# Attention with a ternary feed-forward: output projections of two row blocks to one PSUM bank, and the written order of the attention passes laid out anew

## The reference

```
xn  = layernorm(x)                                  # x: 4 x 2048 x 256
att: q, k, v for 16 heads of 16 (half of q and k rotated by rope), causal softmax over 2048 keys
y   = softmax(q k^T / 4, causal) v                  # 4 x 2048 x 256
ffn: h = gelu(xn @ ternary(W_fc)^T); h = layernorm(h) * ln_w + ln_b; h @ ternary(W_proj)^T
out = x + y @ Wc + ffn
```

## Time and profile before

| | |
|---|---|
| median of three runs | 1917.17 us |
| profiled execution, its own time | 1912.73 us |
| its span, first to last instruction | 1910.9 us |
| TensorE matmul busy | 1832.3 us (96%) |
| VectorE busy | 1678.8 us (88%) |
| ScalarE busy | 1582.8 us (83%) |
| GpSimd busy | 538.3 us (28%) |
| mean granted TensorE clock | 0.972 of full speed |

### The profile page before, as it was taken

How to read it: one execution, slowest core, us unless ns; L and a number is a source line. 1 busy time by engine, 2 the same in 40 slices (tenths; PEclk the granted TensorE clock), 3 DMA queues, 4 the chain that set the end, 5 groups by cost and what they waited for, 6 DMA issues and landing times.

```text
span 1910.9 us, 41847 instructions
## 1 busy us (share of the span) xinstructions
PE 1832.3 (96%) x13879; PEld 695.6 (36%) x13879; DVE 1678.8 (88%) x4770; ACT 1582.8 (83%) x1916; POOL 538.3 (28%) x648
## 2 busy tenths in 40 slices
PE   6899999999879999999999999999999999999998
PEld 6555555565412222222332323222232322323223
DVE  5699999999779898999999999999999999999961
ACT  2477667666339999999999999999999999999994
POOL 0122112112151342415234241432414144241210
PEclk7899999999859999999999999999999999999999
DMA  4133333325333133140414314142341415323112
GB/s 177 32 95 104 88 88 102 106 75 117 102 80 66 22 58 49 31 64 22 81 35 80 58 44 64 44 95 30 72 59 43 67 40 94 43 59 64 35 40 74
DMA packets 160324, 129.01 MB, mean 68 GB/s; under 512 B 95344, under 2 KB 144752, under 8 KB 159768
## 3 DMA queue, kind: packets, MB, share of 16 engines
q1 hardware_dynamic: 160152, 126.88, 30.7%
HBM read 74.60 MB, written 42.98 MB: 62 GB/s over the span
## 4 chain that ended last, share of the span: by engine, by line
PE 45%; ACT 14%; issue 7%; DVE 5%; POOL 1%; SPq 1%; DMA 0%; DVEq 0%; ACTq 0%; POOLq 0%
PE pv L1570 18%; ACT prob L1352 12%; PE st L1555 10%; PE sm L1532 10%; PE sm L1503 4%; PE st L1542 2%; DVE sm L1433 2%; ACT excess L1345 1%; DVE sm L1421 1%; DVE pm L1438 1%; DVE pm L1421 0%; DVE pm L1433 0%; PE sm L1527 0%; ACT Y L1335 0%; POOL apart L1262 0%
## 5 line engine op out<-in xcount | busy, mean ns | idle before, releaser
L1352 ACT ACTIVATE prob<-st 128x1024 f32<-128x1024 f32 x1088 | 1047.7, 1029 | 62.7 <-PE st L1555 53.5
L1570 PE MATMUL pv<-prob,V 128*32 128x512 f32 (+3 forms) x5120 | 589.6, 542 | 5.6 <-POOL prob L1311 5.3
L1421 DVE CUSTOM_DVE_ANT_0 sm<-sm,mask 128x256 f32<-128x256 f32 (+3 forms) x1024 | 473.9, 521 | 39.2 <-PE sm L1532 35.0
L1532 PE MATMUL sm<-K,Q 48*128 48x512 f16 (+3 forms) x2112 | 479.8, 350 | 16.5 <-DVE pm L1421 6.9
L1555 PE MATMUL st<-Q,K 50*128 50x512 f16 (+3 forms) x2560 | 476.9, 353 | 13.9 <-ACT prob L1352 8.3
L1438 DVE TENSOR_REDUCE pm<-sm 128x1 f32<-128x512 f32 x640 | 412.6, 684 | 40.3 <-PE sm L1532 37.0
L1311 POOL TENSOR_SCALAR_AFFINE_SELECT prob<-prob 128x256 f32<-128x256 f32 (+1 forms) x448 | 190.4, 439 | 862.5 <-ACT prob L1352 857.7
L1433 DVE CUSTOM_DVE_ANT_0 sm<-sm,excess 128x512 f32<-128x512 f32 x448 | 301.3, 711 | 16.8 <-PE sm L1532 16.0
L1532 PEld LDWEIGHTS sm<-K,Q 48*128 48x128 f16 x2112 | 151.4, 95 | 325.6 <-DVE pm L1433 109.2
L1555 PEld LDWEIGHTS st<-Q,K 50*128 50x128 f16 x2560 | 125.2, 94 | 370.3 <-ACT prob L1352 270.4
L1345 ACT ACTIVATE excess<-st 128x1024 f32<-128x1024 f32 x218 | 220.6, 1025 | 9.1 <-DVE pm L1438 4.7
(11 more groups left out here) (169 smaller groups left out, 1938.1 us busy)
## 6 DMA issues: line engine op xcount, KB each, us to landing
Q<-scratch_q SPq DMA_DIRECT2D x102, 128.0 KB, 4.2
K<-scratch_k SPq DMA_DIRECT2D x102, 128.0 KB, 7.0
x<-in_x SPq DMA_DIRECT2D x16, 512.0 KB, 4.4
scratch_v<-Rt SPq DMA_DIRECT2D x64, 128.0 KB, 2.0
scratch_r<-Rt SPq DMA_DIRECT2D x16, 512.0 KB, 3.2
V_raw<-scratch_v SPq DMA_DIRECT2D x16, 512.0 KB, 10.0
Yc<-Y SPq DMA_DIRECT2D x124, 64.0 KB
spread<-scratch_i SPq DMA_DIRECT2D x124, 64.0 KB, 2.2
```

What stands on the lines that cost most here:

```text
L1352: act.activation(prob_of(quad, k)[:, :, :], st[number % ST][:, :, :], ACT.Exp).then_inc(exp_done, 1)
L1421: i = dve.tensor_tensor_reduce(x, x, mask[:, CH - block_width(t, k):], 1.0, -3e38, ALU.add, ALU.max, best(h, t, k))
L1532: i = pe.matmul(dst[:, at:at + width], lhsT=Q[slot][r, h // 2, t * P:(t + 1) * P], rhs=K[slot][r, h // 2, k * CH:k * CH + width], start=Tr ...
L1570: i = pe.matmul(pv[2 * DH * h:2 * DH * (h + 1), CH - width:CH], lhsT=V[quad % VSLOTS][:, j, h, :], rhs=prob_of(quad, u)[:, h % 2, at:at + ...
```

## The change

The four project entries of a pass become two: each fills one bank with two blocks of 128 tokens (four fp32 matmuls of 256 columns, eight records in the profile, one start flag per block), and one addition takes all 512 columns. In pass 15 the 16 late entries of chunks 12 to 15 become 8. A pass has 113 entries in place of 115. The order string is another one throughout. At the start of the stage, `load_kc(0)` and `place_ones(0)` go ahead of `load_v(0)`, `load_kc(1)` goes ahead of `load_m(0, 0, 0)`, `load_kc(quad)` waits for the second of the six difference operations of quad - 1 in place of the last, and on GpSimd the clearing of KC goes ahead of that of the ones, the differences of quad 0 ahead of the presetting of V, and the clearing of yn behind the differences of quad 1.

```
-PROJECT_AT = (64, 75, 87, 99)
+PROJECT_AT = (64, 87)
-    for s in reversed(range(SUB)):
-        sequence.insert(PROJECT_AT[s], ("project", s))
+    for a in reversed(range(HALVES)):
+        sequence.insert(PROJECT_AT[a], ("project", a))
-INVERT_EARLY, INVERT_LATE = LATE + 2, PROJECTS[2] + 1
+INVERT_EARLY, INVERT_LATE = LATE + 2, PROJECTS[1] + 1
 TIMETABLE = (
-    "wsmmswxmmwmsmsmmsmmswmmsmxwxmmsmwmxmsmmsmmsmwsmmsmwsmmsmwmxmxmmsmmxw"
-    "msmsmwsmmmxmswsmmsmsmmsmwmsmsmwmmsmswsmmmswxmmswsmmsmwsmmsmwsmsmmxwm"
-    "smmswmsmmswsmmmswxmwmssmmwsmsmmmswsmmswsmmmswsmmswsmmmswsmmswsmsmmms"
-    "wxmmmswsmmswmsmmxwmsmmswxmmms"
+    "wsmmxwmsmwsmmxmxmsmmsmwsmmsmwxmmsmwmmssmwmmsmswmsmmswsmmsmmxmxmxmwms"
+    "mmsmswsmmmswxmmxwmsmmswmsmmswsmmmswsmmswsmmmswsmmsxwsmsmmsmwsmmsmwsmm"
...
-BEHIND = {STEP_AT[TC - 1] + 3 + i: (FIRST_TWO + 2 * i, FIRST_TWO + 2 * i + 1) for i in range(6)}
-for i in range(SUB):
-    n = STEPS - LAG - SUB + i
-    BEHIND[n] = BEHIND.get(n, ()) + (THIRD + i,)
+BEHIND = {STEP_AT[TC - 1] + 3 + i: (FIRST_TWO + i,) for i in range(3 * HALVES)}
+for i in range(HALVES):
+    BEHIND[STEPS - LAG - SUB + 1 + 2 * i] = (THIRD + i,)
...
             def load_kc(quad):
-                sp.wait_ge(differed, quad) if quad else sp.wait_ge(kc_made, 1)
+                sp.wait_ge(apart_steps, 5 * quad - 3) if quad else sp.wait_ge(kc_made, 1)
...
+            sp.wait_ge(ones_made, 1)
+            load_kc(0)
+            place_ones(0)
             load_v(0)
-            sp.wait_ge(ones_made, 1)
-            place_ones(0)
-            load_kc(0)
             load_qk(sp, scr, 1, Q[1], K[1], qk_loaded[1])
             for s in range(1, SLOTS):
                 place_ones(s)
+            load_kc(1)
             load_m(0, 0, 0)
-            load_kc(1)
...
+            pool.memset(KC[:, :, :], 0.0).then_inc(kc_made, 1)
             pool.memset(ones[:, :], SHIFT).then_inc(ones_made, 1)
-            pool.memset(KC[:, :, :], 0.0).then_inc(kc_made, 1)
...
-            pool.memset(yn[:, :, :], 0.0).then_inc(yn_cleared, 1)
+            difference_of_keys(0, 0, 16 * LOADS)
             for s in range(VSLOTS):
                 pool.memset(V[s][:, :, :, DH:2 * DH], 1.0)
-            difference_of_keys(0, 0, 16 * LOADS)
             place_v(0, 0)
             difference_of_keys(1, 1, 16 * LOADS)
+            pool.memset(yn[:, :, :], 0.0).then_inc(yn_cleared, 1)
...
-            def add(quad, slot, e, g, s):
+            def add(quad, slot, e, g, a):
-                dve.tensor_tensor(out=residual(g)[:, s, :], in0=residual(g)[:, s, :], in1=x[:, 0:C], op=ALU.add).then_inc(sm_read, 1)
+                r = residual(g)[:, 2 * a:2 * a + 2, :]
+                dve.tensor_tensor(out=r, in0=r, in1=x[:, :].rearrange("p (s c) -> p s c", s=2), op=ALU.add).then_inc(sm_read, 1)
...
-                t = CH * (g % TC) + P * s
-                for a in range(CC):
-                    r = slice(0, G * DH if others and a == CC - 1 else P)
-                    i = pe.matmul(dst[:, 0:C], lhsT=Yc[g // TC % 2][r, a, t:t + P], rhs=Wc[r, a, :], start=a == 0, stop=a == CC - 1)
+                for s in range(2):
+                    t = CH * (g % TC) + P * (2 * half + s)
+                    for a in range(CC):
+                        r = slice(0, G * DH if others and a == CC - 1 else P)
+                        i = pe.matmul(dst[:, s * C:(s + 1) * C], lhsT=Yc[g // TC % 2][r, a, t:t + P], rhs=Wc[r, a, :],
+                                      start=a == 0, stop=a == CC - 1)
                 i.then_inc(sm_ready, 1)
```

More of the change, by code:

```diff
@@ L767 @@
 LATE = 4
+HALVES = SUB // 2
 LEAD = 7
-PROJECT_AT = (64, 75, 87, 99)
+PROJECT_AT = (64, 87)
 EXCESSES = 3
@@ L826, in half_of @@
     return SEQ[e][1][0][0] % 2
-PROJECTS = [next(e for e in range(NE) if SEQ[e] == ("project", s)) for s in range(SUB)]
-INVERT_EARLY, INVERT_LATE = LATE + 2, PROJECTS[2] + 1
+PROJECTS = [next(e for e in range(NE) if SEQ[e] == ("project", a)) for a in range(HALVES)]
+INVERT_EARLY, INVERT_LATE = LATE + 2, PROJECTS[1] + 1
 WIDE = 2 * CH
@@ L867 @@
 TIMETABLE = (
-    "wsmmswxmmwmsmsmmsmmswmmsmxwxmmsmwmxmsmmsmmsmwsmmsmwsmmsmwmxmxmmsmmxw"
-    "msmsmwsmmmxmswsmmsmsmmsmwmsmsmwmmsmswsmmmswxmmswsmmsmwsmmsmwsmsmmxwm"
-    "smmswmsmmswsmmmswxmwmssmmwsmsmmmswsmmswsmmmswsmmswsmmmswsmmswsmsmmms"
-    "wxmmmswsmmswmsmmxwmsmmswxmmms"
+    "wsmmxwmsmwsmmxmxmsmmsmwsmmsmwxmmsmwmmssmwmmsmswmsmmswsmmsmmxmxmxmwms"
+    "mmsmswsmmmswxmmxwmsmmswmsmmswsmmmswsmmswsmmmswsmmxwsmsmmsmwsmmsmwsmm"
+    "smwsmmsmwsmmmswmsmsmwmmsmswsmmmswsmmswsmmsmmswsmmmswsmmswsmmsmmswxmm"
+    "mswsmmswmxmmxwsmmmsmswxmmms"
 )
@@ L895 @@
 FULL = tokens()
-ROWS_LAST, FIRST_TWO, LAST_BEFORE, THIRD = NE, NE + 1, NE + 1 + 2 * SUB, NE + 1 + 3 * SUB
-TURNED, TURNED_BACK, LAST_OWN = NE + 1 + 4 * SUB, NE + 2 + 4 * SUB, NE + 3 + 4 * SUB
-BEHIND = {STEP_AT[TC - 1] + 3 + i: (FIRST_TWO + 2 * i, FIRST_TWO + 2 * i + 1) for i in range(6)}
-for i in range(SUB):
-    n = STEPS - LAG - SUB + i
-    BEHIND[n] = BEHIND.get(n, ()) + (THIRD + i,)
+ROWS_LAST, FIRST_TWO, LAST_BEFORE, THIRD = NE, NE + 1, NE + 1 + 2 * HALVES, NE + 1 + 3 * HALVES
+TURNED, TURNED_BACK, LAST_OWN = NE + 1 + 4 * HALVES, NE + 2 + 4 * HALVES, NE + 3 + 4 * HALVES
+BEHIND = {STEP_AT[TC - 1] + 3 + i: (FIRST_TWO + i,) for i in range(3 * HALVES)}
+for i in range(HALVES):
+    BEHIND[STEPS - LAG - SUB + 1 + 2 * i] = (THIRD + i,)
 def late_block(e):
-    n, s = divmod(e - FIRST_TWO, SUB)
-    return NCH - TC + (0, 1, 3, 2)[n], s
+    n, a = divmod(e - FIRST_TWO, HALVES)
+    return NCH - TC + (0, 1, 3, 2)[n], a
 LAST = []
@@ L1061, in projected @@
                 return (g + TC) * NE + SM + PROJECTS[-1] + 1
-            return (NQ - 1) * NE + SM + (FIRST_TWO + SUB, FIRST_TWO + 2 * SUB, TURNED, LAST_OWN + 2)[g % TC]
+            return (NQ - 1) * NE + SM + (FIRST_TWO + HALVES, FIRST_TWO + 2 * HALVES, TURNED, LAST_OWN + 2)[g % TC]
         def quads(body):
@@ L1462, in body @@
                         add(quad, slot, e, *late_block(e))
-                        if e == FIRST_TWO + SUB - 1:
+                        if e == FIRST_TWO + HALVES - 1:
                             invert(2 * quad + 1)
@@ L1492, in _, with project @@
         def _(pe):
-            def project(dst, g, s, others=False):
+            def project(dst, g, half, others=False):
                 if g < 0:
```

## The result

The changed kernel takes **1950.34 us** (median of 4 runs, 1950.15 to 1957.28) against 1915.12 us before (4 runs on the same chip, 1910.44 to 1918.38). The ratio is 1.0191, with a 95% interval of 1.0174 to 1.0208: slower by some 35 us, where no measurable change was forecast, and above the forecast's range. The profiled execution took 1950.15 us, with a span of 1948.4.

What follows compares the result with a forecast made beforehand. ScalarE, idling for st that TensorE fills, was taken as the limit. Passes 4 to 15 +6.0, passes 0 to 3 -1.0, start -3.6, last pass +1.2: +2.6 us, so 1919.8; range 1904 to 1934, its own 1911.5 to 1922.9.

Steps and rivals of the forecast that it cites:

- blocks, in place of four single entries: Passes 4 to 15: two projections in a row make gaps of 2.25 us; ScalarE idles 0.5 and 1.0 us.
- the rest of the order: Gaps of a pass without the two blocks: counted excess 3.8 us, so 0.25 us a pass better than before.
- The rule of 1.25 us: Attention passes: where TensorE's work from fill to fill exceeds 1.25 us, ScalarE idles by the rest.
- rival A: Passes 4 to 15: blocks starve ScalarE and VectorE, sm banks free late; +14 us, about 1931; chance 0.31.
- the count: Gaps over 1.25 us in a pass: 36 by 4.5 us in the old order, 34 by 5.8 in the new.
- Dummy passes: Passes 0 to 3, without real projections: only the better order counts, -0.25 x 4 = -1.0 us; 81.8 us each.
- Rival C: TensorE's clock falls in every pass, as it did in passes with dummies; up to +20 us; chance 0.04.
- The start: Start of the stage: earlier key load for quad 1 gains 5.3, later quad 0 loses 1.7; -3.6 us.
- the gain of 6.6 from a still earlier clock: Start of the stage: clock up before the first w; the far end, -6.6 us, not taken.
- The last pass: Pass 15: three "S S S" in place of one, +2.1, stretch begins one S earlier, -0.9; +1.2, ends -1 and +3.
- Larger or smaller operations: VectorE's merged additions: by the skill's rule for unsaturated engines the merge would lose; if saturated, it would win 3.6 us.

Runs made afterwards that it cites:

- split_adj: The changed kernel with each block written as two adjacent entries of four matmuls in two banks, with additions of 256 columns; 1947.52 us.
- split_new: The changed kernel's order and start with four single project entries of four matmuls, at 64, 75, 87 and 99, in place of the two blocks; 1961.58 us.
- after_none: The changed kernel with the projections of the twelve real passes left out, each entry one matmul and one copy of one column; 1960.39 us.
- after_half: The changed kernel with only the first four of the eight matmuls in each real-pass project entry, and additions of 256 columns; 1938.24 us.
- r_early: The changed kernel with the row-maxima entry written two fills earlier in the order, seven fills before the scores that need it in place of five; 1948.08 us.
- after_late2: The changed kernel with LATE at 2 in place of 4, moving only the row-maxima entries; eight fills in place of five before the scores; 1942.52 us.
- spread2: The changed kernel with LATE at 2 and four single project entries of four matmuls, at 64, 76, 87 and 93, in place of the two blocks; 1951.08 us.

## Why the prediction was wrong, by its own steps

A real pass went from 82.43 to 84.84. The runs divide this 2.41:

| part | forecast | shown | by |
|---|---|---|---|
| blocks, in place of four single entries | +0.8 | 1.33 - 0.43 = +0.9 | eight, four and no matmuls; before with and without |
| the rest of the order | -0.25 | +1.5 | both orders without projections |
| sum | +0.5 | +2.4 | |

The division is not the only one, for the two parts aren't independent. In the old order the same blocks, in other places, cost 84.40 - 82.00 = 2.40 us a pass and the merge 1.97; from there the new order adds 0.44 (84.84). The new order has better places for the blocks, as the forecast said (1.33 for 2.40), and is worse by 1.5 in the rest, which the forecast denied. Either way it costs, where it was to win.

*The rule of 1.25 us and the blocks* held: 2.25 us from fill to fill, 0.5 and 1.0 us idle forecast, 0.56 and 1.05 found, and a little taken off the long gap behind (0.34 late with half a block, 0.12 with the whole). VectorE's additions took 0.688 us as forecast, and waited for TensorE as long blocks make them; its starvation, rival A's mechanism, is not what set the time, since the blocks' whole price is the forecast's, and two banks with two short additions in place of one changed nothing. Rival A's 1931 us came nearer for another reason.

*The step that failed* is "without the blocks 3.8, so the rest of the order is 0.25 us better than before". I set the count against what it was to explain again, now by the stretches between the four evacuations of a pass (us by which ScalarE is late, the count by the prediction's prices; found as medians over 14 passes):

| | last to 1st | 1st to 2nd | 2nd to 3rd | 3rd to last |
|---|---|---|---|---|
| before, counted | 0.46 | 1.29 | 1.47 | 1.22 |
| before, found | 0.55 | 1.52 | 1.59 | 1.42 |
| after, counted | 1.32 | 1.98 | 1.10 | 1.33 |
| after, found | 1.14 | 1.95 | 2.32 | 2.11 |

How an entry is priced (0.11 us each, or 0.22 for two side by side and for a single one alike) moves these counts by up to 1 us a pass in all. By either price the third stretch comes out cheaper in the new order and the last within 0.1 us of the old one, and the trace has both dearer by 0.7. It is so with no projection in the pass too: of the order's 1.5 us, 0.8 lie between the second and third evacuation, 0.7 between the third and the last, and nothing in the other two together.

The count is right in the half of the pass that I looked at, where the blocks are, and wrong by 1.2 and 0.8 us in the other two. In the first of these it is the wait for the row maxima (1.11): the rule knows TensorE's own work only, and I never asked of the new order how far each entry stands from what depends on it. The prediction speaks of the row maxima only at the start of the stage. The wait's price is not simply its length: taking it away in the new order gave back 0.35, making it in the old order cost all of it and more. So of the order's 1.5 us a run gives 0.35 to the distance; what makes up the rest of that stretch's 0.8 isn't shown.

In the last stretch no wait is new. A count gap by gap forgets what one gap leaves to the next, as the single entries in empty gaps show (1.32 us late over two gaps where 0.03 and 0.39 are counted); TensorE also waits there for VectorE to free `sm` banks, in both orders. The count agreed with one order to 0.6 us a pass, and I took that as proof for another. Which of the two, carried lateness or banks, makes the 0.7 us of that stretch wasn't tried.

*Dummy passes* were to be 81.8 and were 84.9: 1.5 for the order again, and a clock drop each. Rival C had the clock fall in every pass; it did so in the four dummy passes, in the first for 6.8 us (584.0 to 590.8), where before had three drops of 3.4 us, and in one real pass.

*The start*: -3.6 forecast, -3.0 here, -3.6 in the run of the start alone. The clock, in windows of the kernel after, against the earlier trace rows:

```profile
560.00:570.00 10.00, 9.95 (x45) 2.87 (x43) 7.70 (x28) 8.27 (x10) 3.00 (x7) 0.50 0.04 13
570.00:580.00 10.00, 9.97 (x81) 2.42 (x80) 9.16 (x25) 9.05 (x12) 0.00 (x0) 0.98 0.08 22
```

It was at full speed for nearly all of the second window, where before had 0.83: the rise moved 3 us earlier, as the first w did, and as I took it; the gain of 6.6 from a still earlier clock didn't come.

*The last pass*: +1.2 forecast with an end of +3; +3.4 found. The merge in the old order made it +1.5 (92.17), so some 2 of it are the order's.

*The clock near the end of the span*, windows of the kernel after, 10 us each in pass 12:

```profile
1632.00:1642.00 10.00, 8.08 (x53) 1.94 (x49) 5.68 (x12) 5.67 (x6) 7.45 (x8) 0.67 0.33 94
1642.00:1652.00 10.00, 10.00 (x73) 2.68 (x69) 7.85 (x30) 8.31 (x10) 9.62 (x5) 0.82 0.25 81
```

In that pass the row maxima landed late, and TensorE stood still for 1.92 us:

```profile
1635.56 0.61 PE L1558 MATMUL st<-Q,K 50*128 50x512 f16 x2 [1.92 <-DMA Q<-ml]
```

The clock was at 1.2 GHz for 10.2 us from 1635.3 on, 0.3 us before TensorE went on: 5.0 us lost in one pass, the wait included. The five kernels with five fills between that entry and its use (this one, split_adj, split_new, after_none, after_half) all have a longer third stretch in pass 12 than in the passes around it, by 0.9 to 3.5 us; r_early, after_late2 and spread2, with seven or eight, have not.

*Larger or smaller operations.* VectorE, which isn't saturated, did one addition for two, and its busy time stayed as it was (77.03 for 77.07). The Trainium skill, "Perfetto Trace Analysis", section "Optimizing Scalar/DVE Operations", says that breaking up instructions may let work finish sooner where Scalar or Vector aren't saturated but cause bubbles on other engines. The runs don't bear that out here, nor speak against it: with two additions for one the pass took 84.85 us for 84.84. The bubbles came from TensorE's eight matmuls, of which the rule says nothing, so the prediction reached the right sign by a rule that wasn't at work.

## What to carry to other kernels

Where an order of work is written anew, check for each transfer how much work stands between what starts it and what waits for it, in the old order and in the new, before counting anything else: here it went from seven fills to five and made a wait of 1.1 us where there was none. A count that explains one order proves nothing for another until it is compared stretch by stretch, and short gaps in front of long ones are in use even when they hold nothing. To find what a merge costs, halve it and leave it out, in the old order and in the new; then check the clock before reading any time.

## What the runs showed of the hardware that was not expected

Work left out did not make the kernel faster, and in one order made it slower. With the projections of twelve passes left out the old order took 1921 us in place of 1915 (the interval of the ratio is 1.0005 to 1.0044), the changed one 1960 in place of 1950, there with intervals that touch. TensorE's clock was at 1.2 GHz in all twelve passes of the changed order, for 3.4 to 10.2 us at a time, and in seven of the old. A stretch of 3.4 us costs 1.5 to 1.6 us in the old order, 1.2 to 1.6 in the new. With the real projections the changed kernel runs the same passes at full clock, but for the one in which TensorE stood still for a transfer; the merge in the old order had five drops in real passes, always in the stretch with the second block. Why the clock falls in one and not in the other is open.

A row-maxima load costs SyncE 5 us to issue for eight DMAs, and another 1.06 us pass from the last issue's end until TensorE goes on; once, it was 2.2 us (issue ended at 1633.37, fill at 1635.56), and the clock fell during that wait.
